# New begin times for the steady batch and the last batch of a planned adaLN kernel

## The chip, the cores and the metric

The kernel runs on one core of a Trainium2 chip. The metric is the device time of one execution in microseconds, median of 3 runs. Shorter is better.

## The reference, cut to what matters

The input is 8 batches of 1024 rows of 256 numbers. All of it is float32.

```python
mod = (silu(c) @ wmod).reshape(8, 6, 1, 256)      # sa, ca, ga, sb, cb, gb; |ga|, |gb| at least 0.25
h = layernorm(x) * (1 + ca) + sa
x = x + ga * causal_attention(h)                  # q, k, v by 16 small blocks, rope, softmax over 1024 keys
h = layernorm(x) * (1 + cb) + sb
y = h
for l in range(2):                                # two layers of the inner network
    q, k, v = split(shift_token(y) @ wqkv[l])     # 8 heads of 64
    q, k = xpos(l2norm(q) * qs[l], l2norm(k) * ks[l])
    y = y + window_attention(q, k, v) @ wo[l]     # own and previous 128 rows
    a, g = split(layernorm(shift_token(y)) @ w1[l] + b1[l])
    y = y + (a * gelu(g)) @ w2[l] + b2[l]         # 682 hidden units
x = x + gb * y
```

## The kernel before

The work of a batch is cut into tiles of 128 rows, 8 in a batch and 16 over its two layers. A **piece** is a short run of instructions of one kind on one engine for one tile, head group, pair of tiles or block of hidden units, and there are 9244 of them. The kinds that the text needs:

- `E` (TensorE, L508 and L514): one of the three 512-wide parts of q, k, v of a tile, six float16 matmuls. `ev` (ScalarE, L779) copies it out of PSUM. `Wg` and `Wa` (L613, L617) are the matmuls of the hidden layer, `J` (L594, L598) those of `wo`, `Y` (L160 to L162, L638) those of `w2`.
- `F` (L524) transposes q and k, float32 over all 128 rows of the array. `G` (L547, scores), `H` (L565, transposes of the probabilities) and `I` (L581, probabilities times v) are float32 matmuls that go to a part of the array, 64 rows or 64 columns of it.
- `x0` and `x1` (VectorE, L1079 and L1086): the two products of the position rotation, 128x1024, both operands in SBUF. `nm` (L1111, L1117) divides half of the probabilities by their sum, SBUF only. `ss` (L1054, L1059) sums squares. `yr` (L1183, and in layer 2 also L1188 and L1190) adds the result of `Y` to the residual; it is the last piece of a tile in a layer.
- `ad` (GpSimd, L1370) adds the two products, 128x1024. `pw` (L1366) raises a 128x16 block to the power -1/2, `kk` (L1376) scales k, 128x512, and `ul` (L1385) makes the low half of a hidden block, 128x512.
- `ex` (ScalarE, L808) and `pe` (L730) are exponentials, `ge` (L855) is the gelu. Going from one to the other loads another table.
- SyncE's queue issues all DMAs of the steady batches: `xl` loads two tiles of x (L310), `xs` writes shifted rows (L335, L337), `mb` and `mg` load gates, `os` stores a tile (L341).

The order of the pieces isn't written as a program. `BEGIN` holds a begin time for each piece of a batch, and a piece of batch b begins b times `PERIOD` later. `EDGE` replaces that time for single pieces of single batches, and `ONCE` holds the pieces of the set-up. `schedule()` sorts all pieces by time, engine by engine. That gives each engine its queue. At run time nothing waits for a clock: an engine takes the next piece of its queue as soon as the semaphores that the piece waits for have been counted up. A semaphore's target is the rank of the awaited piece in its own queue (`at()`). `plan_banks()` gives each TensorE piece the PSUM bank whose last use ends first by the same times, and TensorE waits for that use to end (`claim()`).

```python
time_b = round(time + b * PERIOD, 2)
made.append((EDGE.get((k, engine), {}).get(piece[1:], time_b), engine, piece))
```

In the steady state the queues hold two batches at once: the causal attention of batch b+1 lies among the pieces of the second layer of batch b.

Of the kernel before, what the change touches and what calls it, by code (L numbers as in the profile page):

```python
# [46 lines left out]
def adaln_kernel(nc, x, w_q, w_k, w_v, wqkv, q_scale, k_scale, wo, ln_g, ln_b, w1, b1, w2, b2,  # L47
# [3 lines left out]
    with ExitStack() as ctx:  # L51
# [1342 lines left out]
PERIOD = 316.98  # L1394
BEGIN = {
# [525 lines left out]
```

How the kernel before makes its waits and increments, by code:

```python
        def claim(pe, *use):  # L275
            for old in before[use]:
                pe.wait_ge(*empty(old))
            return bank[use]
# [12 lines left out]
        def root(pool, ve, mv, rs, lo, hi, s_eps, count):  # L292
            pool.tensor_scalar(ve[:, lo:hi], mv[:, lo:hi, 1], EPS, None, ALU.add).then_inc(s_eps, 1)
            pool.wait_ge(s_eps, count)
            return pool.tensor_tensor(rs[:, lo:hi], ve[:, lo:hi], neg_half[:, 0:hi - lo], ALU.pow)
# [5 lines left out]
            @block.sync  # L302
            def _(sp):
                for piece in ORDER["sp"]:
                    k = piece[0]
                    if k == "xl":
                        b, p = piece[1:]
                        if b:
                            sp.wait_ge(s_fin, (b - 1) * NT + 2 * p + 2)
                        sp.dma_start(X[:, 2 * p:2 * p + 2, :],
                                     x[b, 2 * p * P:(2 * p + 2) * P, :].rearrange("(t p) d -> p t d", p=P)
                                     ).then_inc(s_x[p], 16)
                    elif k == "mb":
                        b = piece[1]
                        if b:
                            sp.wait_ge(s_u0, at("lr", b - 1, NT - 1))
                        else:
                            sp.wait_ge(l_store, 16)
                        sp.dma_start(modb[:, :, :],
# [3 lines left out]
                        b = piece[1]  # L323
                        if b:
                            sp.wait_ge(s_fa, b * NT)
                        else:
```

## Time and profile before

| | us |
|---|---|
| median of 3 runs | 2638.1 |
| lowest and highest run | 2637.03, 2639.17 |
| span of the profiled execution | 2634.1 |
| TensorE busy in the span | 2526.7 |
| VectorE busy in the span | 2260.9 |
| ScalarE busy in the span | 1935.6 |
| GpSimd busy in the span | 1303.7 |

The span goes from the first to the last instruction of the profiled execution. The profile gives no device time of that execution beside its span. The median of the timed runs is 4.0 us above the span, and that is taken for what lies around it. Busy times of TensorE are modelled at their ends and overlap a little, so they say less than the starts of its instructions.

### The profile page before, as it was taken

How to read it: one execution, taken by the hardware profiler on the slowest of the kernel's cores; microseconds unless marked ns; L12 is line 12 of the kernel's file. 1: busy time of each engine (PE TensorE's matmuls, PEld its weight loads, DVE VectorE, ACT ScalarE, POOL GpSimd, SP SyncE). 2: the span in 40 equal slices, each digit the busy share in tenths (PEclk: the TensorE clock that was granted, in tenths of full speed). 3: DMA queues.
4: the chain of work that ended last, by engine and by line, in shares of the span. 5: the costliest groups of instructions: out<-in, count | busy, mean ns of one | idle time of the engine just before them, and what ended most of it. 6: DMA issues, size and time to landing. Idle time of an engine off the chain costs nothing.

```text
span 2634.1 us, 71297 instructions
## 1 busy us (share of the span) xinstructions
PE 2526.7 (96%) x25566; PEld 1725.1 (65%) x25566; DVE 2260.9 (86%) x6247; ACT 1935.6 (73%) x4782; POOL 1303.7 (49%) x953
## 2 busy tenths in 40 slices
PE   7899989999899998999999999999999999999998
PEld 4566666666567665676656666666766666666675
DVE  8997889878898788987889878998889978799785
ACT  3698856888478784788748787587874878658884
POOL 2364535555355554555436554365544555446552
PEclk8999999999999999999999999999999999999999
DMA  5000010000100000000000000000000000000000
GB/s 192 22 7 8 5 43 3 9 5 15 33 3 9 6 17 30 4 10 4 18 29 5 8 5 20 25 6 8 6 19 25 6 8 6 20 25 6 7 6 21
DMA packets 51021, 46.45 MB, mean 18 GB/s; under 512 B 11530, under 2 KB 47980, under 8 KB 50548
## 3 DMA queue, kind: packets, MB, share of 16 engines
q1 hardware_dynamic: 50004, 40.78, 5.0%
q8 instruction: 213, 3.49, 0.6%
q14 instruction: 132, 1.08, 0.1%
q10 hardware_dynamic: 672, 1.10, 0.1%
HBM read 25.06 MB, written 8.42 MB: 13 GB/s over the span
## 4 chain that ended last, share of the span: by engine, by line
PE 69%; DVE 12%; ACT 8%; issue 5%; POOL 4%; DMA 1%; SPq 1%; DVEq 0%; POOLq 0%; ACTq 0%
PE ps L508 10%; PE ps L613 9%; PE ps L581 8%; PE ps L547 6%; PE ps L514 5%; PE ps L617 4%; PE ps L565 4%; PE ps L524 3%; PE ps L594 3%; PE ps L160 2%; PE ps L162 2%; PE ps L161 2%; ACT ar_b L808 2%; PE ps L461 2%; PE ps L407 2%
## 5 line engine op out<-in xcount | busy, mean ns | idle before, releaser
L808 ACT ACTIVATE ar_b<-ar_b,small 128x192 f32<-128x192 f32 (+1 forms) x1024 | 445.2, 437 | 50.4 <-DVE small L1100 48.6
L1366 POOL TENSOR_TENSOR small<-small,neg_half 128x16 f32<-128x16 f32 x128 | 382.2, 2986 | 121.8 <-DVE small L1059 119.9
L1370 POOL TENSOR_TENSOR ar_c<-ar_c 128x1024 f32<-128x1024 f32 x128 | 302.7, 2365 | 282.3 <-DVE ar_c L1086 281.7
L1100 DVE CUSTOM_DVE_ANT_0 ar_b<-ps,mask_t,small 128x192 f32<-128x192 f32 x896 | 319.3, 413 | 29.7 <-PE ps L547 29.2
L1385 POOL TENSOR_TENSOR mlp<-mlp 128x512 f16<-128x512 f32 x160 | 196.3, 1231 | 200.5 <-ACT mlp L863 199.3
L508 PE MATMUL ps<-wqkv_hi,ht_hi 128*128 128x512 f16 x768 | 292.2, 381 | 0.0
L508 PE MATMUL ps<-wqkv_lo,ht_hi 128*128 128x512 f16 x768 | 291.1, 379 | 0.0
L613 PE MATMUL ps<-ht_hi,w_hi 128*128 128x512 f16 (+1 forms) x704 | 268.2, 381 | 5.5 <-ACT ht_hi L759 5.5
L613 PE MATMUL ps<-ht_hi,w_lo 128*128 128x512 f16 (+1 forms) x704 | 267.1, 379 | 0.0
L581 PE MATMUL ps<-ar_b,ar_a 128*64 128x128 f32 x3840 | 239.4, 276 | 0.5 <-DVE ar_b L1124 0.3
L294 POOL TENSOR_SCALAR stats<-stats 128x2 f32<-128x2 f32 x128 | 33.2, 260 | 407.6 <-DVE stats L1149 312.5
L514 PE MATMUL ps<-wqkv_hi,ht_lo 128*128 128x512 f16 x768 | 228.4, 379 | 0.0
L581 PEld LDWEIGHTS ps<-ar_b,ar_a 128*64 128x64 f32 x3840 | 207.2, 137 | 29.7 <-issue 17.4
L617 PE MATMUL ps<-ht_lo,w_hi 128*128 128x512 f16 (+1 forms) x704 | 209.9, 380 | 0.0
L1176 DVE SCALAR_TENSOR_TENSOR mlp<-ps,bias,mlp 128x512 f32<-128x512 f32 x192 | 142.5, 749 | 70.1 <-PE ps L617 33.1
L819 ACT ACTIVATE ar_b<-ar_b,rsw 128x192 f32<-128x192 f32 (+1 forms) x512 | 193.7, 441 | 11.2 <-DVE rsw L1111 10.2
L547 PE MATMUL ps<-ar_a 64*64 64x64 f32 (+2 forms) x5536 | 196.7, 282 | 2.8 <-ACT ar_a L798 2.8
L1124 DVE COPY ar_b<-ps 128x512 f32<-128x512 f32 (+1 forms) x256 | 160.2, 648 | 44.1 <-PE ps L565 44.1
L808 ACT ACTIVATION_READ_ACCUMULATOR ar_b<-ar_b,small 128x1 f32 x1024 | 193.4, 189 | 0.0
L547 PEld LDWEIGHTS ps<-ar_a 64*64 64x64 f32 x5536 | 153.4, 133 | 40.0 <-issue 22.6
L160 PE MATMUL ps<-w_hi,mlp 128*128 128x256 f16 x640 | 175.4, 274 | 0.2 <-POOL mlp L1385 0.2
L162 PE MATMUL ps<-w_hi,mlp 128*128 128x256 f16 x640 | 175.1, 274 | 0.0
(193 smaller groups left out, 6673.3 us busy)
## 6 DMA issues: line engine op xcount, KB each, us to landing
xu<-in_L_attn_x_dram SPq DMA_DIRECT2D x32, 256.0 KB, 2.8
out_dram<-xu SPq DMA_DIRECT2D x64, 128.0 KB, 2.4
rows<-xu SPq DMA_DIRECT2D x128, 63.5 KB
mlp<-in_L_ffn_wqkv_dram SPq DMA_DIRECT2D x2, 1536.0 KB, 6.4
modb<-mod_rows SPq DMA_DIRECT2D x8, 384.0 KB, 4.5
rows<-in_L_ffn_w_dram SPq DMA_DIRECT2D x2, 1364.0 KB, 9.5
rows<-xu SPq DMA_DIRECT2D x112, 0.5 KB
ar_b<-in_L_wmod_dram SPq DMA_DIRECT2D x2, 768.0 KB, 7.4
```

The costliest lines, as they stand in the source:

```text
L160: pe.matmul(o, a[0], b[0], start=start, stop=False)
L162: return pe.matmul(o, a[1], b[0], start=False, stop=stop)
L508: pe.matmul(ps[:, bk, :], ht[0][:, c, a:a + P], wqkv_p[i][:, L % DEPTH, c, s * INNER:(s + 1) * INNER], start=(c == 0 and i == 0), stop=False)
L514: last = pe.matmul(ps[:, bk, :], ht[1][:, c, a:a + P], wqkv_p[0][:, L % DEPTH, c, s * INNER:(s + 1) * INNER], start=False, stop=(c == 1))
L547: last = pe.matmul(ps[HQ * half:HQ * half + HQ, bk[q], i * KW + o:i * KW + o + m], QT[r:r + HQ, n % 2, hp, HQ * half:HQ * half + HQ], KT[r ...
L581: last = pe.matmul(ps[64 * q:64 * q + 64, bk, (h // 2) * P:(h // 2 + 1) * P], V[:, (n - 1 + kb) % 4, h * DH:(h + 1) * DH], PTW[:, f, q, 2 ...
L613: pe.matmul(ps[0:m, bk, :], q[:, L % DEPTH, c, 2 * j + i, 0:m], ht[0][:, c, a:a + 512], start=(c == 0 and q is w1_p[0]), stop=False)
L617: last = pe.matmul(ps[0:m, bk, :], w1_p[0][:, L % DEPTH, c, 2 * j + i, 0:m], ht[1][:, c, a:a + 512], start=False, stop=(c == 1))
L808: last = act.activation(pw, pw, ACT.Exp, bias=mnw[:, n % 2, h:h + 1], scale=-1.0, accum_out=smw[:, n % 2, h:h + 1])
L1100: dve.tensor_tensor_reduce(out=PW[:, pw_at(f, q, i) + c:pw_at(f, q, i) + KW], in0=ps[:, bk, i * KW + c:(i + 1) * KW], in1=mask, scale=rinv ...
L1366: pool.tensor_tensor(rinv[:, n % 4, :], ssm[:, n % 2, :], neg_half[:, 0:16], ALU.pow).then_inc(s_rinv, 1)
L1370: pool.tensor_tensor(M1[:, n % 2, :], M1[:, n % 2, :], M2, ALU.add).then_inc(s_add, 1)
```

## The change

All begin times are replaced: `PERIOD`, `BEGIN`, `ONCE` and `EDGE`. The set of pieces, the functions and the instructions in each piece stay as they are. The old tables begin at -30.17, the new ones at 0. `EDGE` had 709 times, all for the first batch and the first part of the second, and now has 2575, for the first batch, much of the second and the last one.

Sorted by time, the two tables give these queues. In the first batch they are the same up to the new time 328: the first 291 pieces of TensorE, 325 of ScalarE, 339 of VectorE, 106 of GpSimd and 32 of SyncE don't move. In a steady batch 252 of TensorE's 316 pieces and 296 of VectorE's 356 stand in another place among those of their batch, by at most 25 places, and in the last batch 268 and 313. SyncE's stores `os` stood together behind the four `xl` of the next batch, and now most of them stand between those.

The core of the diff (`EDGE` has keys with all numbers of a piece, `BEGIN` those within a batch):

```diff
-PERIOD = 316.98
+PERIOD = 320.36
 BEGIN = {
...
-    ("mg", "sp"): {(): 152.68},
...
-    ("os", "sp"): {0: 345.6, 1: 346.12, 2: 346.64, 3: 347.16, 4: 347.68, 5: 348.2, 6: 348.72, 7: 349.24},
...
-    ("xl", "sp"): {0: -23.25, 1: -1.62, 2: 23.79, 3: 28.11},
...
-    ("yr", "dve"): {0: 159.25, 1: 160.25, 2: 180.65, 3: 182.5, 4: 220.94, 5: 222.55, 6: 226.86, 7: 240.7, 8: 289.53,
-        9: 291.44, 10: 307.79, 11: 313.97, 12: 338.13, 13: 339.38, 14: 342.32, 15: 343.7},
...
+    ("mg", "sp"): {(): 72.74},
...
+    ("os", "sp"): {0: 337.97, 1: 340.58, 2: 356.01, 3: 358.81, 4: 386.82, 5: 389.25, 6: 390.55, 7: 393.53},
...
+    ("xl", "sp"): {0: 20.6, 1: 38.83, 2: 69.26, 3: 73.55},
...
+    ("yr", "dve"): {0: 204.11, 1: 205.81, 2: 211.51, 3: 223.3, 4: 265.83, 5: 267.94, 6: 270.01, 7: 273.27, 8: 336.56,
+        9: 339.17, 10: 354.6, 11: 357.4, 12: 385.41, 13: 387.84, 14: 389.14, 15: 392.12},
...
 EDGE = {
...
-    ("x0", "dve"): {(0,): 53.47, (1,): 63.85, (2,): 83.24, (3,): 93.24, (4,): 99.35, (5,): 117.53, (6,): 136.13,
-        (7,): 143.72, (8,): 171.4, (9,): 177.69, (10,): 195.38},
...
-    ("yr", "dve"): {(0,): 160.5, (1,): 161.12, (2,): 183.17, (3,): 183.5},
...
+    ("x0", "dve"): {(0,): 93.25, (1,): 104.41, (2,): 125.18, (3,): 135.67, (4,): 141.9, (5,): 160.49, (6,): 179.15,
+        (7,): 186.86, (8,): 215.69, (9,): 222.11, (10,): 239.86, (11,): 261.56, (12,): 276.17, (13,): 286.85,
...
+    ("yr", "dve"): {(0,): 205.16, (1,): 205.62, (2,): 227.38, (3,): 227.84, (4,): 265.96, (5,): 267.71, (6,): 272.06,
+        (7,): 285.69, (8,): 336.57, (9,): 339.18, (10,): 354.62, (11,): 357.41, (12,): 385.43, (13,): 387.85,
+        (14,): 389.15, (15,): 392.13, (16,): 524.38, (17,): 526.18, (18,): 531.88, (19,): 543.67, (20,): 586.2,
...
+        (31,): 712.49, (116,): 2511.26, (117,): 2513.96, (118,): 2529.58, (119,): 2530.74, (120,): 2590.5,
+        (121,): 2593.05, (122,): 2596, (123,): 2597.95, (124,): 2615.73, (125,): 2617.6, (126,): 2619.47,
+        (127,): 2621.34},
```

What else can be counted in the two sets of tables, before and after:

| counted in the tables | before | after |
|---|---|---|
| steps on TensorE from a piece of another kind to `G`, `H` or `I`, steady batch | 32 | 45 |
| the same in the interval of the last batch, and in all | 32, 257 | 51, 356 |
| table loads on ScalarE, steady batch, last batch, all | 14, 12, 112 | 12, 6, 94 |
| `nm`, `x0`, `x1` that overlap a `kk` or `ul` by the tables, steady batch | 14 | 6 |
| `nm`, `x0`, `x1` that overlap a `pw` by the tables, steady batch | 19 | 22 |

## Rows read from the trace of the kernel before

**Rows 1.** The page: span, busy time of each engine and the granted TensorE clock in 40 slices.
```profile
span 2634.1 us, 71297 instructions
...
PE 2526.7 (96%) x25566; PEld 1725.1 (65%) x25566; DVE 2260.9 (86%) x6247; ACT 1935.6 (73%) x4782; POOL 1303.7 (49%) x953
...
PEclk8999999999999999999999999999999999999999
```

**Rows 2.** The page: the chain of waits that ended last, share by engine.
```profile
PE 69%; DVE 12%; ACT 8%; issue 5%; POOL 4%; DMA 1%; SPq 1%; DVEq 0%; POOLq 0%; ACTq 0%
```

**Rows 3.** Windows, one steady batch and the last: PE, PEld, DVE, ACT, POOL, clock, DMA.
```profile
1348.00:1669.00 321.00, 311.06 (x3163) 212.30 (x3161) 278.12 (x774) 239.44 (x595) 162.85 (x118) 0.99 0.05 13
...
2311.00:2634.00 323.00, 305.54 (x3090) 207.20 (x3090) 262.20 (x720) 231.95 (x578) 155.17 (x109) 0.98 0.04 13
```

**Rows 4.** Timeline of VectorE: `x0` of tiles 0 and 8, then `yr`: start, duration.
```profile
91.23 1.23 DVE L1079 TENSOR_TENSOR ar_c<-ar_b,xp_t 128x1024 f32<-128x1024 f32 x1
...
211.55 1.22 DVE L1079 TENSOR_TENSOR ar_c<-ar_b,xp_t 128x1024 f32<-128x1024 f32 x1 [0.23 <-ACT ar_b L779]
...
281.60 0.41 DVE L1183 TENSOR_TENSOR xu<-ps,xu 128x256 f32<-128x256 f32 x1
...
281.93 0.16 DVE L1111 RECIPROCAL rsw<-small 128x4 f32<-128x4 f32 x1
...
385.68 0.42 DVE L1183 TENSOR_TENSOR xu<-ps,xu 128x256 f32<-128x256 f32 x1
...
2310.43 0.42 DVE L1183 TENSOR_TENSOR xu<-ps,xu 128x256 f32<-128x256 f32 x1
...
2630.57 0.42 DVE L1183 TENSOR_TENSOR xu<-ps,xu 128x256 f32<-128x256 f32 x1 [0.51 <-PE ps L638]
```

**Rows 5.** Timeline of VectorE and GpSimd at 1149 us.
```profile
1149.16 1.42 DVE L1117 TENSOR_TENSOR ar_b<-ar_b,rsw 128x384 f32<-128x384 f32 x1
...
1149.00 1.15 POOL L1385 TENSOR_TENSOR mlp<-mlp 128x512 f16<-128x512 f32 x1 [0.38 <-ACT mlp L863]
...
1150.12 3.23 POOL L1366 TENSOR_TENSOR small<-small,neg_half 128x16 f32<-128x16 f32 x1
```

**Rows 6.** Timeline of VectorE and GpSimd at 1138 us.
```profile
1138.33 1.23 DVE L1079 TENSOR_TENSOR ar_c<-ar_b,xp_t 128x1024 f32<-128x1024 f32 x1
...
1139.47 1.24 DVE L1079 TENSOR_TENSOR ar_c<-raw,xp_t 128x1024 f32<-128x1024 f32 x1
...
1138.41 3.91 POOL L1366 TENSOR_TENSOR small<-small,neg_half 128x16 f32<-128x16 f32 x1 [5.33 <-DVE small L1059]
```

**Rows 7.** By source line: durations in ns, least, median and most.
```profile
L1117 DVE TENSOR_TENSOR ar_b<-ar_b,rsw x256: 424/558/1419, 121.4 to 2586.5; 128x384 f32<-128x384 f32 x112, 128x256 f32<-128x256 f32 x16
...
L1385 POOL TENSOR_TENSOR mlp<-mlp x160: 1149/1159/2061, 184.2 to 2619.5; 128x512 f16<-128x512 f32 x160
...
L1366 POOL TENSOR_TENSOR small<-small,neg_half x128: 2892/2910/3907, 108.1 to 2560.4; 128x16 f32<-128x16 f32 x128
```

**Rows 8.** Groups by line and shape: busy us, mean ns of one.
```profile
L1117 DVE TENSOR_TENSOR ar_b<-ar_b,rsw 128x384 f32<-128x384 f32 x224 | 144.4, 644 | 7.8 <-DVE rsw L1111 0.2
```

**Rows 9.** Timeline of TensorE: where pieces `E` and what follows begin.
```profile
1414.20 0.38 PE L508 MATMUL ps<-wqkv_hi,ht_hi 128*128 128x512 f16 x1
...
1415.59 0.59 PE L565 MATMUL ps<-id_f,ar_b 64*128 64x64 f32 x12
...
1447.53 0.38 PE L508 MATMUL ps<-wqkv_hi,ht_hi 128*128 128x512 f16 x1
...
1448.82 0.38 PE L508 MATMUL ps<-wqkv_hi,ht_hi 128*128 128x512 f16 x1
...
1450.12 1.05 PE L524 MATMUL ps<-id_f,ar_c 128*128 128x128 f32 x8
```

**Rows 10.** By source line: the table loads that stand before `ge`.
```profile
L855 ACT ACT_TABLE_LOAD  x56: 1283/1283/1283, 176.4 to 2602.9; - x56
```

**Rows 11.** Waits of SyncE's queue: for whom, us in total, times, longest.
```profile
SPq L335 <- DVE xu L1136: 1952.9, 120, 65.1
```

More of the change, by code:

```diff
@@ L1391 @@
 BY_LAYER = ("D", "N", "Wg", "Wa", "dh", "dl", "nh", "nl", "ls", "lt", "lk", "ge", "us", "uh", "ul")
-PERIOD = 316.98
+PERIOD = 320.36
 BEGIN = {
[203 rows of a table removed]
[204 rows of a table added]
 }
 ONCE = {
-    ("bw", "pe"): {(0, 0): -7.46, (0, 1): 2.64, (0, 2): 8.25, (0, 3): 12.59, (1, 0): 40.81, (1, 1): 45.54,
-        (1, 2): 47.41, (1, 3): 48.84},
-    ("co", "act"): {(0,): -15.41, (1,): 27.89},
-    ("cq", "act"): {(0, 0): 2.68, (0, 1): 6.61, (1, 0): 45.3, (1, 1): 70.45},
-    ("cv", "act"): {(0,): -0.64, (1,): 46.67},
-    ("cw", "act"): {(0, 0): -6.21, (0, 1): 0.82, (1, 0): 31.73, (1, 1): 51.89},
-    ("do", "dve"): {(0,): -13.19, (1,): 29.82},
-    ("dq", "dve"): {(0, 0): 6.25, (0, 1): 8.34, (1, 0): 50.99, (1, 1): 103.49},
-    ("dv", "dve"): {(0,): 1.11, (1,): 85.3},
-    ("dw", "dve"): {(0, 0): 10.54, (0, 1): 21.57, (1, 0): 36, (1, 1): 60.87},
-    ("z0", "dve"): {(): -30.17},
-    ("zM", "pe"): {(): -21.4},
-    ("zR", "pe"): {(): -23.65},
-    ("zT", "pe"): {(): -27.43},
-    ("zW", "pe"): {(): -18.05},
-    ("za", "act"): {(): -30.17},
-    ("zb", "sp"): {(): -5.02},
-    ("zc", "sp"): {(): -29.7},
-    ("zd", "act"): {(): -22.56},
-    ("ze", "act"): {(): -26.54},
-    ("zf", "dve"): {(0,): 19.32, (1,): 53.25},
-    ("zg", "sp"): {(): -21.69},
-    ("zh", "act"): {(): -18.51},
-    ("zi", "dve"): {(): -26.32},
-    ("zk", "dve"): {(): -19.57},
-    ("zl", "dve"): {(): -17.64},
-    ("zm", "sp"): {(): -7.6},
-    ("zn", "dve"): {(): -17.81},
-    ("zo", "sp"): {(0,): -26.98, (1,): -26.5},
-    ("zp", "dve"): {(): -22.56},
-    ("zq", "sp"): {(0,): -7.3, (1,): 10.18},
-    ("zr", "act"): {(): -11.57},
-    ("zs", "sp"): {(): 10.7},
-    ("zt", "dve"): {(): -10.36},
-    ("zu", "dve"): {(): -20.44},
-    ("zv", "sp"): {(0,): -25.48, (1,): 16.46},
-    ("zw", "sp"): {(0,): -26.02, (1,): 23.63},
-    ("zx", "sp"): {(): -6.78},
-    ("zy", "dve"): {(0,): 31.55, (1,): 44.52},
-    ("zz", "dve"): {(): 79.71},
@@ new lines @@
+    ("bw", "pe"): {(0, 0): 24.44, (0, 1): 35.88, (0, 2): 42.36, (0, 3): 46.53, (1, 0): 76.74, (1, 1): 82.64,
+        (1, 2): 85.68, (1, 3): 88.28},
+    ("co", "act"): {(0,): 15.82, (1,): 63.1},
+    ("cq", "act"): {(0, 0): 37.32, (0, 1): 41.26, (1, 0): 82.28, (1, 1): 110.79},
+    ("cv", "act"): {(0,): 33.52, (1,): 83.76},
+    ("cw", "act"): {(0, 0): 28.48, (0, 1): 35.22, (1, 0): 69.39, (1, 1): 92.52},
+    ("do", "dve"): {(0,): 22.38, (1,): 65.6},
+    ("dq", "dve"): {(0, 0): 41.37, (0, 1): 43.29, (1, 0): 88.48, (1, 1): 146.27},
@@ new lines @@
+    ("dv", "dve"): {(0,): 35.71, (1,): 127.38},
+    ("dw", "dve"): {(0, 0): 45.77, (0, 1): 57.23, (1, 0): 71.78, (1, 1): 101.22},
+    ("z0", "dve"): {(): 0},
+    ("zM", "pe"): {(): 12.54},
+    ("zR", "pe"): {(): 11.04},
+    ("zT", "pe"): {(): 6.88},
+    ("zW", "pe"): {(): 16.04},
+    ("za", "act"): {(): 0},
+    ("zb", "sp"): {(): 32.11},
+    ("zc", "sp"): {(): 0.43},
+    ("zd", "act"): {(): 8.96},
+    ("ze", "act"): {(): 8.66},
+    ("zf", "dve"): {(0,): 54.92, (1,): 92.75},
+    ("zg", "sp"): {(): 8.48},
@@ new lines @@
+    ("zh", "act"): {(): 14.97},
+    ("zi", "dve"): {(): 9.07},
+    ("zk", "dve"): {(): 13.76},
+    ("zl", "dve"): {(): 16.67},
+    ("zm", "sp"): {(): 27.03},
+    ("zn", "dve"): {(): 16.32},
+    ("zo", "sp"): {(0,): 3.07, (1,): 3.55},
+    ("zp", "dve"): {(): 10.49},
+    ("zq", "sp"): {(0,): 27.33, (1,): 45.32},
+    ("zr", "act"): {(): 22.32},
+    ("zs", "sp"): {(): 45.97},
+    ("zt", "dve"): {(): 24.42},
+    ("zu", "dve"): {(): 12.16},
+    ("zv", "sp"): {(0,): 4.48, (1,): 52.77},
+    ("zw", "sp"): {(0,): 4.03, (1,): 59.44},
@@ L1643 @@
+    ("zx", "sp"): {(): 27.98},
+    ("zy", "dve"): {(0,): 67.43, (1,): 80.76},
+    ("zz", "dve"): {(): 121.28},
 }
 EDGE = {
[153 rows of a table removed]
[466 rows of a table added]
 }
```

1005 rows, old and new, of tables (BEGIN, EDGE) are left out of this document.

## Prediction

> **What bounds the kernel now.** I read the page first. Of the span of 2634.1 us TensorE is busy for 2526.7, at the higher of its two clock levels (2.4 GHz) in nearly every slice after the first, and VectorE for 2260.9 [rows 1]. The chain of waits says how much of the end each engine sets: TensorE 69%, VectorE 12%, ScalarE 8%, GpSimd 4% [rows 2]. The windows show that a steady batch keeps TensorE busy for 311 of 321 us and VectorE for 278, and that the last interval is less dense on all engines (305.5 and 262.2 of 323) though it is as long [rows 3]. So the kernel is near TensorE's own work in the middle and has room at its end.
>
> Then I compared the trace with the old table, by the begin of `yr` of a batch's last tile. The trace has it at 385.68 in batch 0, at 2310.43 in batch 6 and at 2630.57 in batch 7 [rows 4]. The period is (2310.43 - 385.68)/6 = 320.79 us, where the old table says 316.98. The old table is 3.81 us or 1.20% too quick per batch. The last interval is 2630.57 - 2310.43 = 320.14, and 3.5 us of span follow.
>
> **What the new table's own times are worth.** No instruction is added or removed, so the change is queues, bank choice and nothing else. The new table gives each piece a time, and that can be tested on the trace of before, because the first batch's queues are the same up to about 328. The new table has `x0` of tile 0 at 93.25, of tile 8 at 215.69, and `yr` of tile 7 at 285.69. The trace has them at 91.23, 211.55 and 281.60 [rows 4]. So the trace is 2.0, 4.1 and 4.1 us ahead of the new table. The old one (with its offset of 30.17) gives 83.64 and 270.87 for the first and the last of these, 7.6 and 10.7 us too early: it loses 3.1 us in 190.4, 1.63%, and 1.20% in the steady state. The new table gains 2.1 in 190.4, 1.1%, all of it before 212. One reason is visible: after `yr` of tile 7 VectorE begins the next instruction 0.33 us later [rows 4], the old table's shortest such step is 0.33 and the new one's is 0.46. The new table is a little slow on VectorE.
>
> **The sum.** It goes by four stretches of the span.
> 1. To `yr` of tile 15: 392.13 in the new table, less the lead of 4.1, is 388.0. Before it was 385.7. The 2.3 us are paid because the second batch's attention is interleaved otherwise near the end of batch 0.
> 2. Six periods of 320.36 plus an error d. The lead shows d between 0 (the flat stretch from tile 8 to `yr` 7) and -1.1% or -3.5 us (the whole stretch). I take the middle, -1.8, since either stretch is part of a batch.
> 3. The last interval: 2621.34 - (392.13 + 6 x 320.36 = 2314.29) = 307.05, against 320.14 before. By the same half rate that is -1.7. The gain of 13 us is the largest single term, and the room for it is in [rows 3].
> 4. The tail of 3.5 us stays.
>
> What the new table doesn't charge: a step from another kind to `G`, `H` or `I`. In the trace `E` at 1447.53 is followed by `E` at 1448.82 and by `F` at 1450.12, 1.29 and 1.30 us, but `E` at 1414.20 by `H` only at 1415.59, 1.39 us [rows 9]. The new table gives all of these 1.30. The same undercharge is in the calibrated first batch with its 32 to 35 such steps, so only the added ones count: 13 in a steady batch, 19 in the last. At 0.095 us, and with TensorE on 69% of the chain [rows 2], that is +0.85 and +1.25.
>
> So d = -1.8 + 0.85 = -0.95, a period of 319.4. Total: 388.0 + 6 x 319.4 + (307.05 - 1.7 + 1.25 = 306.6) + 3.5 = 2614.5 us of span, 19.6 less than before. With the 4.0 us between span and median this is 2618.5, and I say 2619 us, 0.72% faster. Carrying no lead forward at all (d = +0.85, last 308.3) gives 2621.9 + 4.0 = 2626. This end, too, is faster.
>
> **The contention.** `nm` at 1149.16 takes 1.42 us while `ul` runs on GpSimd from 1149.00 for 1.15, and the `pw` behind it, begun at 1150.12, takes 3.23 [rows 5]. The medians are 0.56 and 2.91 [rows 7]. `nm` of the 384-wide form has a mean of 644 against a median of 558 ns, 0.086 x 224 = 19.3 us in all or 2.4 per batch [rows 7, 8]. By the tables 14 of the `nm`, `x0` and `x1` of a batch overlap a `kk` or `ul` before, and 6 after. If all of 2.4 went and all lay on the path, a period would lose 2.4; if only VectorE's 12% share counted, 0.3. I take none of it on top: the first batch, on which the table was tested, had such stretches in its measured times, and the table's 320.36 already supposes them gone. That the steady state has fewer than the batch it is tested on speaks for the lower half of my range.
>
> Here a rule of the Trainium skill is to be weighed, from the page "SBUF — State Buffer", section "SBUF: two separate sides": VectorE with two SBUF inputs and GpSimd share a port pair as an exclusive lock for the whole instruction, and who comes second fully blocks. For `ul` and `nm` the trace agrees: `nm` starts 0.16 after `ul` and takes 0.86 more than its median, about the rest of `ul`. For `pw` it doesn't: `x0` at 1139.47 runs wholly inside a `pw` begun at 1138.41 and takes 1.24 us, its usual time; it is `pw` that takes 3.91 instead of 2.91, having begun behind another `x0` [rows 6, 7]. By the rule the change would keep its worst case, since overlaps of `nm`, `x0` and `x1` with `pw` go from 19 to 22 in a batch. By the trace they cost VectorE nothing and `pw` at most 1.0 us each.
>
> **Edits that I cost at nothing.** The shift of all times by 30.17 changes no queue. Two table loads fewer per steady batch and six fewer in the last take 2 x 1.28 and 6 x 1.28 us off ScalarE [rows 10], but the new times have them already; uncovered they would be worth 8% of that. SyncE's stores go ahead of loads in its queue. A store waits for the `yr` that the load behind it also waits for, and the queue mostly idles (1952.9 us before the `xs` alone, [rows 11]), so the load loses one issue. If the cover goes, it is `st` and the first LayerNorm of the next batch that are late, by about a microsecond per batch, +7 in all. `mg` waits for the whole previous batch and stands before the last `xl` now. What is queued behind it waits for nearly the same `yr`. Bank waits change everywhere, and I have no row for them; they cost between nothing and the late case of the first rival.
>
> **Rivals.**
> - *TensorE is the bound and its undercharge is paid in full: slower.* All 45 steps to `G`, `H`, `I` cost 0.095, 4.3 us per batch, and nothing that the table overcharges gives it back: period 324.6, last interval 307.05 + 51 x 0.095 = 311.9, total 388.0 + 1947.6 + 311.9 + 3.5 + 4.0 = 2655. For it: 311 of 321 busy. Against it: the first batch has the same undercharge and is ahead of the table all the same. It decides from an error of +1.9 us in each of the seven intervals, where the gain is gone: (2634.1 - 388.0 - 1922.2 - 307.05 - 3.5)/7.
> - *The queues don't do what the table says: no change.* Engines start when semaphores allow, orders tuned to times that are off by a per cent meet waits that the table hasn't, and the tail keeps its length of 320: 388.0 + 6 x 320.4 + 320 + 3.5 + 4.0 = 2638. For it: the old table missed its last interval by 3 us and each period by 3.8.
> - *The table is slow everywhere.* The lead grows by 1.1% in every batch: period 320.36 - 3.5 + 0.85 = 317.7, last 307.05 - 3.4 + 1.25 = 304.9, total 388.0 + 1906.2 + 304.9 + 7.5 = 2607. For it: the old table did better in the steady state (1.20%) than in the tested stretch (1.63%).
> - *Full blocking at `pw`*, each `pw` shutting out VectorE's SBUF pieces: three more overlaps per batch and 1.7 us more of them by the tables, on the path at most 1.7 x 8 = 14 us, so 2626 + 14 = 2640. Against it stands [rows 6]. The Trainium skill page "SBUF — State Buffer" would have it so.
>
> **Chances.** My forecast (2612 to 2631) 0.55; the slow table, down to 2600, 0.18; no change 0.14; TensorE bound 0.10; blocking 0.03. A measurement of this kernel tells 0.2% (5.3 us) from no change. Faster: 0.55 + 0.18 and a share of the rest, 0.76. Same: 0.13. Slower: 0.11. The range of 2602 to 2640 leaves out the TensorE case and the far end of the slow-table case; the forecast's own range is 2612 to 2631.
>
> **What would show it.** In the profile after, `yr` of tile 15 near 388, batches 319 to 320 us apart, the last interval near 307, the mean of L1117 near its median, and 94 table loads. `E` before `H` should still take 1.39. Wrong would be a period over 322.3, or a last interval over 315; then I should look at what TensorE waits for.

## The result, and the profile after

| | before | after |
|---|---|---|
| median of 4 runs, us | 2637.6 | 2820.7 |
| ratio, 95% interval | | 1.0695 [1.0679, 1.071] |
| `yr` of tile 15, batch 0 | 385.68 | 395.33 |
| period, batches 1 to 6 | 320.8 | 348.6 |
| last interval | 320.1 | 329.7 |

The change makes the kernel 7% slower. I had said 0.7% faster, and 2820.7 lies far outside the range of 2602 to 2640. The error of 202 us is the first batch (+7.3), six periods of 348.6 where 319.4 was said (+175), the last interval (+23), and 3 us less around the span than I took.

The page of after, as [rows 1] and [rows 2]:

```profile
span 2819.9 us, 71279 instructions
...
PE 2587.5 (92%) x25566; PEld 1725.6 (61%) x25566; DVE 2359.5 (84%) x6247; ACT 1930.4 (68%) x4764; POOL 1320.7 (47%) x953
...
PEclk8999999999999999999999999999999999999999
...
PE 57%; DVE 23%; issue 8%; DMA 6%; ACT 3%; POOL 2%; SPq 1%; DVEq 0%; POOLq 0%; ACTq 0%
```

The matmuls and VectorE's counted instructions are the same in number, but VectorE is busy 98.6 us longer and TensorE 60.8. VectorE holds 23% of the chain instead of 12, and DMA 6% instead of 1.

The windows of after, one steady batch and the last interval, as [rows 3], with the same columns:

```profile
1440.50:1788.30 347.80, 318.80 (x3161) 212.16 (x3161) 292.28 (x773) 239.49 (x593) 165.55 (x118) 0.99 0.04 12
2486.70:2816.40 329.70, 307.66 (x3079) 203.96 (x3078) 269.20 (x711) 223.27 (x568) 152.47 (x106) 0.99 0.03 9
```

TensorE idles 29 us in a steady batch, where it was 10. VectorE does its work of a batch in 292 us and not 278: instructions that don't wait in the queue take longer.

VectorE's timeline of after, `yr` of the last tile of batches 0, 6 and 7, as [rows 4]:

```profile
395.33 0.42 DVE L1183 TENSOR_TENSOR xu<-ps,xu 128x256 f32<-128x256 f32 x1
...
2486.70 0.42 DVE L1183 TENSOR_TENSOR xu<-ps,xu 128x256 f32<-128x256 f32 x1
...
2816.38 0.42 DVE L1183 TENSOR_TENSOR xu<-ps,xu 128x256 f32<-128x256 f32 x1 [0.51 <-PE ps L638]
```

**First reading: a wait that I had not priced.** VectorE's waits, for whom, us in total, times, longest. After:

```profile
DVE stats L1145 <- DMA rows<-xu: 68.5, 36, 4.7
```

Before:

```profile
DVE stats L1145 <- DMA rows<-xu: 8.8, 17, 2.0
```

L1145 is the second half of `ls`, the statistics of the inner LayerNorm for two tiles. It reads the rows that `xs` has shifted. VectorE's timeline of after at such a place, start, duration, wait in brackets:

```profile
1612.75 0.42 DVE L1136 TENSOR_TENSOR xu<-ps,xu 128x256 f32<-128x256 f32 x1
1613.20 0.49 DVE L1142 BATCH_NORM_STATS2 stats<-xu 128x6 f32<-128x128 f32 x2
1618.35 0.49 DVE L1145 BATCH_NORM_STATS2 stats<-rows 128x6 f32<-128x128 f32 x2 [4.66 <-DMA rows<-xu]
```

and SyncE's queue in the same microseconds:

```profile
1613.19 0.60 SPq L335 DMA_DIRECT2D rows<-xu  x1
```

The residual `jr` (L1136) ends at 1613.17, `xs` is issued at once, and the rows can be read at 1618.35, 5.2 us behind `jr`. The trace of before has the same time: its 17 waits at L1145 end 5.16 to 5.26 us behind the last `jr`, the 36 of after 5.16 to 5.66. By the old table the least distance from the second `xs` to `ls` is 4.71 us in a steady batch. By the new one four of eight are well below it: 2.51, 2.52, 3.91 and 4.20. The new table moves `ls` nearer to its DMA than the DMA takes, and VectorE stands.

**Second reading: SBUF pieces of VectorE under `ad`.** VectorE's timeline of after, three places:

```profile
1479.31 1.31 DVE L1059 TENSOR_SCALAR small<-small 128x16 f32<-128x16 f32 x1
...
1505.57 2.38 DVE L1039 SCALAR_TENSOR_TENSOR xu<-xu,stats,modb 128x256 f32<-128x256 f32 x1
...
1517.17 2.73 DVE L1117 TENSOR_TENSOR ar_b<-ar_b,rsw 128x384 f32<-128x384 f32 x1
```

GpSimd's timeline of after, the same places:

```profile
1478.23 2.36 POOL L1370 TENSOR_TENSOR ar_c<-ar_c 128x1024 f32<-128x1024 f32 x1 [9.83 <-DVE ar_c L1086]
...
1505.15 2.52 POOL L1370 TENSOR_TENSOR ar_c<-ar_c 128x1024 f32<-128x1024 f32 x1 [4.41 <-DVE ar_c L1086]
...
1517.13 2.36 POOL L1370 TENSOR_TENSOR ar_c<-ar_c 128x1024 f32<-128x1024 f32 x1 [8.28 <-DVE ar_c L1086]
```

L1059 (the clip behind the sums of squares) takes 0.17 us elsewhere, L1039 (the last step of a LayerNorm's output) 0.48 and L1117 0.56. Each began while an `ad` (L1370) ran and ended 0.03 to 0.41 us behind its end. I summed, over all groups of VectorE instructions of one line and shape, what each takes above the median of its group. This **stretch** is 141 us in after and 49 in before: L1117 45.6 (before 19.3), L1059 32.7 (8.4), L1039 26.6 (0.5), L1016 9.3 and L1190 6.1 (both 0). Not all of it is `ad`'s. Put down to the GpSimd instruction that ran beside each, 84 us of the 141 fall to `ad` (before 9), and L1016 and L1190 were stretched beside two other GpSimd pieces, the subtraction `hl` (L1343) and the addition `ra` (L1348). In each steady batch seven instructions are blocked by `ad` for over half a microsecond, at the same places every time: three L1059, two L1039 and two L1117. With smaller ones that makes 12.2 us a batch, where it was 1.2. The prediction weighed `nm` (L1117) under `ul` and `pw`. It never asked about `ad`.

**Third reading: TensorE pays for a wait twice.** L1039 at 1505.57 is such a block, and TensorE waits for it. TensorE's timeline of after around it:

```profile
1504.73 0.38 PE L508 MATMUL ps<-wqkv_lo,ht_hi 128*128 128x512 f16 x1
...
1508.00 0.72 PE L407 MATMUL ps<-id_f,xu 128*128 128x128 f32 x4 [2.46 <-DVE xu L1039]
...
1510.12 0.63 PE L508 MATMUL ps<-wqkv_lo,ht_hi 128*128 128x512 f16 x1
```

Windows of TensorE there (stretch, length, busy, granted clock and DMA):

```profile
1508.00:1509.60 1.60, 1.60 (x12) 0.64 0.00 0
1509.70:1512.00 2.30, 2.30 (x8) 0.53 0.03 7
1512.00:1516.00 4.00, 4.00 (x28) 1.00 0.00 0
```

TensorE had been busy for 4.5 of the 7.9 us up to 1507.9, with 2.46 us of idling at their end. Behind that the granted clock is 0.64 and then 0.53, about the lower of the two levels (1.2 GHz), and a matmul of 0.38 us takes 0.63. That is part of TensorE's 60.8 us. It doesn't follow each time: behind the same stall of 2.46 us at 812.7 the granted clock stays at 1.00. Over the whole span the clock is 0.978, where it was 0.987. An estimate from these two shares is 0.022 x 2819.9 - 0.013 x 2634.1 = 28 us of full-speed time, if TensorE was at work in all of it.

### The profile page after: what moved, and what is told of

It is laid out like the page before. It is cut to its first block, busy times and chain, and to the rows that moved or that the text cites. A ratio compares the mean times of both kernels' runs of the same rounds, so it can differ in the third digit from the quotient of the medians.

```text
span 2819.9 us, 71279 instructions
## 1 busy us (share of the span) xinstructions
PE 2587.5 (92%) x25566; PEld 1725.6 (61%) x25566; DVE 2359.5 (84%) x6247; ACT 1930.4 (68%) x4764; POOL 1320.7 (47%) x953
## 4 chain that ended last, share of the span: by engine, by line
PE 57%; DVE 23%; issue 8%; DMA 6%; ACT 3%; POOL 2%; SPq 1%; DVEq 0%; POOLq 0%; ACTq 0%
PE ps L613 10%; PE ps L581 7%; PE ps L508 6%; DMA rows<-xu 5%; PE ps L617 5%; PE ps L547 4%; PE ps L565 4%; PE ps L594 3%; PE ps L514 3%; PE ps L524 2%; PE ps L160 2%; PE ps L162 2%; PE ps L161 2%; PE ps L461 2%; DVE ar_c L1086 2%
## 5 line engine op out<-in xcount | busy, mean ns | idle before, releaser
L1370 POOL TENSOR_TENSOR ar_c<-ar_c 128x1024 f32<-128x1024 f32 x128 | 304.9, 2382 | 455.3 <-DVE ar_c L1086 454.2
L581 PE MATMUL ps<-ar_b,ar_a 128*64 128x128 f32 x3840 | 247.0, 278 | 6.5 <-ACT ar_b L827 6.1
L565 PE MATMUL ps<-id_f,ar_b 64*128 64x64 f32 x3840 | 167.7, 228 | 41.3 <-DVE ar_b L1117 20.4
L565 PEld LDWEIGHTS ps<-id_f,ar_b 64*128 64x128 f32 x3840 | 139.6, 139 | 105.7 <-DVE ar_b L1117 53.9
L1117 DVE TENSOR_TENSOR ar_b<-ar_b,rsw 128x384 f32<-128x384 f32 (+1 forms) x256 | 184.7, 721 | 9.1 <-DVE rsw L1111 0.4
```

The costliest lines, as they stand in the source:

```text
L565: last = pe.transpose(ps[:, bk[half], o:o + HQ], PW[r:r + HQ, c:c + P], id_f[r:r + HQ, r:r + HQ])
L581: last = pe.matmul(ps[64 * q:64 * q + 64, bk, (h // 2) * P:(h // 2 + 1) * P], V[:, (n - 1 + kb) % 4, h * DH:(h + 1) * DH], PTW[:, f, q, 2 ...
L1370: pool.tensor_tensor(M1[:, n % 2, :], M1[:, n % 2, :], M2, ALU.add).then_inc(s_add, 1)
```

## The experiments

The base was measured beside each group of runs, at 2638.8 to 2640.1. Most edits were put into the new kernel and, as a control, into the old one. All figures are medians of 4 to 10 runs. What a run is less than after is taken from the one median of 2820.7, measured beside a base of 2637.6, so such a difference is uncertain by 2 or 3 us.

### The wait for the shifted rows

In `stats_u` the second half of `ls` reads the unshifted columns, and the wait moves to `lk`, the next reader. The shift's part in the statistics is left out.

```diff
-                        dve.wait_ge(s_xs[l * 4 + p], 16 * (4 - (p == 0)) * (b + 1))
...
-                            last = dve.bn_stats(stw[:, w, 1, :], XS[:, w, :])
+                            last = dve.bn_stats(stw[:, w, 1, :], U[:, w, P:DIM])
...
+                        dve.wait_ge(s_xs[L % DEPTH * 4 + p], 16 * (4 - (p == 0)) * (L // DEPTH + 1))
```

> The kernel after, but ls takes the second half of its statistics from U instead of the shifted rows (so the sums are of other numbers), waits for no DMA, and lk waits for the rows instead, at least 2.1 us later in the table. Queues unchanged. DMA-wait theory: VectorE stops 68.5 us in all before L1145 because seven of eight ls lie less than 5.5 us behind their xs; most of that goes and the time falls by 60 to 140 us, to 2680 to 2760. Lock theory (small SBUF pieces of VectorE shut out by GpSimd's ad): the blocked 141 us of VectorE stay, and the time falls by 10 us at most. TensorE theory (more steps to G, H, I): no change within 5 us.

> The same edit on the kernel before, as the control. VectorE stops 8.8 us in all before L1145 there, so the DMA-wait theory gives 0 to 9 us less, 2629 to 2638; the others give no change.

Measured 2774.7 in the new kernel, 46.0 less, and 2635.4 in the old one, ratio 0.9983 [0.9974, 0.9992]. The stretch in the new kernel stays at 144 us. So the wait is real and about a quarter of the loss of 183 us (a part of it may only have moved to `lk`); my figure for it was too high.

The mirror of it puts only the early `ls` into the old table, and leaves nothing out:

```diff
+    for L in range(NB * DEPTH):
+        for p in range(NT // 2):
+            t = when["xs", L * NT + 2 * p + 1][0] + 2.5
+            when["ls", L, p][0] = min(when["ls", L, p][0], round(t, 2))
```

> The kernel before with each ls set to at most 2.5 us behind its second xs (old table: 4.7 to 11.6), nothing else. DMA-wait theory: about eight stops of 2.2 us or more per batch on VectorE, 18 us per batch, of which 12% (VectorE's share of the chain before) to all is paid: 2655 to 2780. Lock theory and TensorE theory: within 5 us of 2638.

Measured 2783.6, 1.0536 [1.0519, 1.0554]: 144 us lost by the place of one kind of piece. Its waits:

```profile
DVE stats L1145 <- DMA rows<-xu: 119.8, 64, 2.9
```

That is 111 us more than before, and the stretch stays (45 us). In VectorE's queue each `ls` of a steady batch stands 1 to 11 places further ahead. So a microsecond of VectorE's standing costs more than a microsecond here (144 for 111).

The other way round, `ls` a little later in the new table, to 4.9 us behind `xs` where the place of `lt` (GpSimd, the next step of the same LayerNorm) allows it:

```diff
...
+            t = when["xs", L * NT + 2 * p + 1][0] + 4.9
+            lt, ls = when["lt", L, p], when["ls", L, p]
+            ls[0] = max(ls[0], min(round(t, 2), round(lt[0] - 0.02, 2)))
```

> The new kernel, whole, with one change of order: where the planned time from the second xs to ls is under 4.9 us, ls begins later, up to 4.9 us behind xs but ahead of lt's planned time (in the steady batch four of eight ls move, by 0.2 to 1.25 us; the others keep their place). Theory A: VectorE does other pieces in some of the time that it stood waiting, 5 to 35 us less than after. Rival B: each ls still waits, for lt's planned time caps the shift, and the time stays within 5 us.

Measured 2821.3, the time of after. Its waits are unchanged:

```profile
DVE stats L1145 <- DMA rows<-xu: 67.5, 36, 4.7
```

This run tests neither theory, for its edit does nearly nothing. Only the order counts at run time, and sorted by time the two queues of VectorE differ in one exchange in the whole run (`ls` and `yr` next to each other in batch 0) and in no steady batch; the other four queues are the same. The new begin times pass no other piece. It is in effect a second measurement of after, 0.6 us from the first. Whether an `ls` that is really placed later wins something back in the new order was not tried.

### The block under `ad`

`ad` on 64 of its 1024 columns. The second product of the rotation is left out in the others.

```diff
-                        pool.tensor_tensor(M1[:, n % 2, :], M1[:, n % 2, :], M2, ALU.add).then_inc(s_add, 1)
+                        pool.tensor_tensor(M1[:, n % 2, 0:64], M1[:, n % 2, 0:64], M2[:, 0:64], ALU.add).then_inc(s_add, 1)
```

> The new kernel with `ad`, GpSimd's rotary addition, on 64 of its 1024 columns, so that the long instruction of 2.36 us (L1370) that VectorE's small pieces stood under becomes a short one; the other 960 columns stay without the second rotary product. Theory A (the wait of ls for the shifted rows and the block by ad add up to most of the slowdown): VectorE's stretch over its usual durations falls from 141 to about 60 us and the time falls by 60 to 120 us, to 2700 to 2760. Rival B (the wait for the rows and the delay it hands on are the cause, and the block by ad is hidden): the time falls by no more than 20, to 2800 or above. The control before_ad_short says what the shorter work alone gives.

> The control: the same cut of ad to 64 columns in the kernel before. Theory A: VectorE's stretch there is 49 us and only part of it under ad, so 0 to 15 us less than before. Rival B: the same; if it falls by over 30, the cut is worth something by itself and the fall of after_ad_short has to be read against it.

Measured 2753.3 in the new kernel, 67.5 less, and 2643.1 in the old one, 1.0012 [1.0003, 1.0022]. In the old order the shorter work gives nothing. The source lines in the new kernel with short `ad`, with least, median and greatest duration in ns:

```profile
L1039 DVE SCALAR_TENSOR_TENSOR xu<-xu,stats,modb x64: 483/485/487, 53.2 to 2487.5; 128x256 f32<-128x256 f32 x64
```
```profile
L1059 DVE TENSOR_SCALAR small<-small x128: 174/175/222, 108.4 to 2681.9; 128x16 f32<-128x16 f32 x128
```

The same lines in after:

```profile
L1039 DVE SCALAR_TENSOR_TENSOR xu<-xu,stats,modb x64: 483/485/2396, 54.0 to 2550.7; 128x256 f32<-128x256 f32 x64
```
```profile
L1059 DVE TENSOR_SCALAR small<-small x128: 174/175/1843, 108.7 to 2751.1; 128x16 f32<-128x16 f32 x128
```

The stretch falls from 141 to 55 us, with nothing left under `ad` but 0.3 us a batch. Of the terms that were taken out, this is the largest. The edit does two things at once: it takes the block away, and it makes `ad` itself 2.0 us shorter (0.32 us in place of 2.36) for what waits for its sum. In the old order neither is worth anything; how the 67.5 us divide between them in the new order was not separated. That the block as such reaches TensorE is seen at 1508.00, where TensorE waits for a blocked L1039, and in the next run, which leaves `ad` as it is.

One victim alone, the clip L1059, is taken out; it is all that is left out:

```diff
-                        dve.tensor_scalar(ssm[:, n % 2, :], ss[:, n % 2, :], 1e-24, None, ALU.max).then_inc(s_rm, 1)
-                        pool.tensor_tensor(rinv[:, n % 4, :], ssm[:, n % 2, :], neg_half[:, 0:16], ALU.pow).then_inc(s_rinv, 1)
+                        pool.tensor_tensor(rinv[:, n % 4, :], ss[:, n % 2, :], neg_half[:, 0:16], ALU.pow).then_inc(s_rinv, 1)
```

> The new kernel without the clip at L1059 (ss clipped from below at 1e-24), a VectorE piece of 0.17 us that was stretched by 32.7 us in sum over the run (before: 8.4); pw reads the sums directly. It leaves out the clip alone. Theory A: 15 to 45 us less, since the stretch of this piece goes with it and 128 pieces of 0.17 us (22 us) too. Rival B: 10 us less or fewer. Rival C: no change, the block moves to the piece that then stands at that place.

> The kernel before without the clip at L1059; it leaves out the clip alone. It is the control of after_noclip, which came out 24 us under the new kernel, and a candidate for a version below both. The piece was stretched by 8.4 us in sum in before, and 128 x 0.17 = 22 us of VectorE's work go with it, most of it beside TensorE: 2 to 12 us less, 2627 to 2637. If TensorE alone sets the period here, 0.

Measured 2796.8 in the new kernel, 23.9 less, and 2637.6 in the old one, 0.9995 [0.9986, 1.0005]. 128 instructions of 0.17 us are worth nothing in the old order, where they were stretched by 8.4 us in all, and 24 us in the new one, where it was 32.7, most of it under `ad` (28). The stretch falls by 31 us, so the block doesn't move to the next piece.

### Both, and what is left

> The new kernel with both causes taken out at once: ls reads its second half from U's own tile (no wait for the shifted rows) and ad is cut to 64 columns. Theory A: the two account for nearly all of the slowdown, 2640 to 2680. Rival B (there is a third cause, such as TensorE's own work standing too close in the new table): 2700 or above.

Measured 2705.3: 115.5 less than after, and 46.0 + 67.5 = 113.5, so the two add up. But 2705 is not 2640 to 2680: there is more. VectorE's timeline of this kernel shows a part, a wait that has only moved:

```profile
1549.87 0.28 DVE L1148 BATCH_NORM_AGGREGATE stats<-stats 128x2 f32<-128x12 f32 x2
1554.21 0.35 DVE L1158 TENSOR_SCALAR rows<-xu,stats 128x128 f32<-128x128 f32 x1 [4.06 <-issue]
```

`lk` (L1158) now waits for the same rows; their `jr` ended at 1548.94, again 5.3 us earlier. So `lk` too was made to read the unshifted columns:

> The new kernel with ad on 64 of 1024 columns, ls and lk both reading U's own columns (the copy of shifted rows is still issued, and only yr, at least 15 us later, asks for it). It leaves out the shift by one row and most of ad. In after_both, where only ls had stopped waiting for the rows, VectorE still stood 4.1 us in each steady batch ahead of an lk. Theory A (that wait is the remainder of the wait for the rows and holds up TensorE): 25 to 40 us less than after_both, 2665 to 2680. Rival B (it lies beside TensorE's work, and a third cause holds the rest): within 10 us of after_both, 2695 to 2710.

Measured 2701.2, 4 less, where I had expected 25 to 40. Those 4 us per batch lay beside TensorE's work. Then all long GpSimd pieces but `pw` were cut (the others from the second batch on):

> The same, and from the second batch on all of GpSimd's long pieces are short: hl on 32 of 256 columns, ra, ad and ul on 64 columns, kk on one head of eight; pw stays as it is. It leaves out those columns of the subtractions, additions and products. With it nothing of GpSimd's can stand under VectorE for long and no row is awaited. Theory A (contention and the rows are all of the slowdown, the new table's spacing is otherwise sound): 2610 to 2650, near the prediction's 2619. Rival B (TensorE's spacing in the new table costs by itself): 2660 or above.

> The control, the same edit in the kernel before, which had 52 us of VectorE stretch, only part of it under these pieces, and 9 us of waits for rows. Theory A: 10 to 30 us less than before, 2608 to 2628, so that the two tables come within 30 us of each other. Rival B: the same here, and the new table stays over 40 us above it.

Measured 2678.3 and 2626.6. The stretch is 21 us in both, and VectorE's work of a steady batch is the same (275.7 and 274.5 us), yet the new table is still 51.7 us behind. Its period is 327.7, where the old table has 319.8 (319.5 in the batch shown). Windows of a steady batch, first the new kernel, then the old one, both with this edit:

```profile
1377.50:1705.20 327.70, 314.26 (x3160) 211.20 (x3160) 275.73 (x773) 239.27 (x593) 87.97 (x118) 0.99 0.04 13
```
```profile
1347.80:1667.30 319.50, 310.51 (x3160) 212.72 (x3160) 274.47 (x773) 239.65 (x595) 87.28 (x118) 0.99 0.05 13
```

In these batches the new table keeps TensorE busy 3.8 us longer, and idle 4.4 us longer. Part of the first is what the prediction called the undercharge. TensorE's timeline of the new kernel with this edit, an `E` and the `H` after it:

```profile
1599.68 0.39 PE L508 MATMUL ps<-wqkv_hi,ht_hi 128*128 128x512 f16 x1
...
1601.09 0.72 PE L565 MATMUL ps<-id_f,ar_b 64*128 64x64 f32 x16
```

That is 1.41 us where the new table has 1.30 (it was 1.39 in [rows 9]). The old table gives this step 1.39, so there it is planned for. In a steady batch 48 steps, nearly all to or from `G`, `H` and `I`, take 0.07 to 0.13 us longer than the new table has them, 4.3 us in sum.

How much of TensorE's own time counts was measured by taking some away: the second of two matmuls of the third product of `Wg` for half of the blocks, 12 of 88 per batch.

```diff
-                        for c in range(NC):
+                        some = k == "Wg" and j < 3
+                        for c in range(NC - some):
```

> after_no_xs_pool with 12 of the 88 L617 matmuls of each batch left out besides (the second half of the third product of Wg for three of its six column blocks), 12 x 0.379 = 4.5 us less of TensorE's work per batch, 36 in all. In after_no_xs_pool 48 steps of a steady batch from one kind of piece to G, H or I took 0.09 us longer than the table has them, 4.3 us per batch. Theory C (with the other causes out, TensorE's own work sets the period, so that this undercharge is paid in full and stays): 30 to 36 us less, 2642 to 2648. Rival D (waits between engines set the period, and TensorE's undercharge lies beside them): under 18 less, over 2660.

> The control, the same 12 matmuls per batch out of before_no_xs_pool. Theory C has the old table bound by TensorE at least as much (311 of 320 us busy), so 25 to 36 less, 2591 to 2602. Rival D: under 18 less.

Measured 2661.4 and 2608.9: 16.9 and 17.7 less.

What these are to be held against isn't the 36.4 us that I had expected from a duration of 0.379. Matmuls overlap, and the time that one takes from TensorE is the distance from start to start. TensorE's timeline of the new kernel before this edit:

```profile
1499.77 0.38 PE L613 MATMUL ps<-ht_hi,w_hi 128*106 128x512 f16 x1
1499.98 0.38 PE L613 MATMUL ps<-ht_hi,w_lo 128*106 128x512 f16 x1
...
1501.07 0.38 PE L613 MATMUL ps<-ht_hi,w_hi 128*128 128x512 f16 x1
```

One matmul begins 0.21 us behind the other, and a piece of six takes 1.30 us. The pieces that lost one take 1.08. So the 96 matmuls are 96 x 0.216 = 20.7 us of TensorE, and 0.82 and 0.85 of that came off the time. With 0.216 theory C reads 17 to 21 us in the new kernel and 14 to 21 in the old one, and rival D under 10. The runs (16.9 and 17.7) lie at the edge of C and in it, though by the bounds as they were written they would be D's. So with the row waits and long GpSimd pieces out, most of TensorE's own time is paid in either table, and the undercharge is worth about 4.3 x 0.82 = 3.5 us per batch (an estimate from this run).

### The last interval

The old tables up to the new time 2446, and from there the new one, shifted by 69.0; the computation is whole.

```diff
+    for q, (time, g) in new.items():
+        made.append((round(time - 69.0, 2) if time > 2446.0 else old[q][0], g, q))
```

> The old tables up to the new time 2446 and the new table, 69 us earlier, behind that: the last batch alone is set anew. If the new last batch keeps what its times say, the gain of 13 us is there: 2625. If waits and locks eat it as in the steady batches (lock and DMA-wait theory), 2633 to 2650: the last interval after was 329.7 against 320.1 before, of which its first part is the steady table's.

Measured 2640.8, 0.9999 [0.999, 1.0008]. Only what begins behind 2446 is moved, the last 175 us; by the tables the end comes 10.2 us earlier with it. The last interval is 321.3 us long, where before has 320.1. VectorE waits in it for shifted rows for 6.8 us (before 2.8), once for 4.7. The two kernels without row waits and long GpSimd pieces say the same of the whole interval: 314.2 us with the new table and 314.3 with the old one. The denser order wins nothing on the chip.

## Why the prediction was wrong

| kernel | us | below after | stretch |
|---|---|---|---|
| after | 2820.7 | | 141 |
| no clip | 2796.8 | 23.9 | 110 |
| `ls` doesn't wait for the rows | 2774.7 | 46.0 | 144 |
| `ad` short | 2753.3 | 67.5 | 55 |
| both of the last two | 2705.3 | 115.5 | 54 |
| and `lk` doesn't wait | 2701.2 | 119.6 | 54 |
| and `hl`, `ra`, `kk`, `ul` short | 2678.3 | 142.4 | 21 |
| the same in before | 2626.6 | | 21 |

- **The step that failed: the worth of the new times.** I took a table whose first batch the trace kept within 4.1 us as right for the steady state, to within d between 0 and -3.5. The steady batches have other queues than the first, so that test said nothing of their distances. The period came out 29.2 above what was said. With row waits and long GpSimd pieces out it was 327.7, so 20.9 of the 29.2 went with these two (and with the shorter work of GpSimd that the edit brings along), and 8.3 are left with the table itself. The error d, put at 0 to -3.5 and with 0.85 added, is the term of the sum that was wrong: it came out at +28.2.
- **What stood in its place, first:** the wait for the shifted rows. It had no term in the sum. One look at the distance from each `xs` to its `ls` in both tables, beside the 5.2 us that the trace of before already shows, would have found it. I counted order changes of SyncE's queue and not the landing of its DMAs.
- **Second: contention.** The prediction had the right mechanism at `ul` and the right finding at `pw` (after it too, `x0` isn't stretched there), but counted only `nm`, `x0` and `x1` against `kk`, `ul` and `pw`. What the change worsened is VectorE's SBUF pieces against `ad`, `nm` among them: 12.2 us of stretch in a steady batch. By the new table, with the offsets and durations that the trace shows, they overlap with `ad` for about 1.5 us a batch (an estimate), and by the old one for 0.8. The mean of the 384-wide L1117 was to come near its median of 0.56 us; it rose from 0.644 to 0.685. A piece put close to an `ad` of 2.4 us tips into it when one of the two is late by little; that is argued from the tables and the timeline, and no run moved such a piece alone. The rows' wait isn't needed for it: the stretch stays at 144 us when `ls` no longer waits.
- **The Trainium skill's rule** ("SBUF — State Buffer", section "SBUF: two separate sides"), of one exclusive lock per instruction and the second to come blocked in full, holds at `ad`: 2.38 us for a 0.48 us piece with two inputs in SBUF, ended 0.28 behind the `ad`. I had seen it hold at `ul` and fail at `pw`, and then gave a chance (0.03) to blocking at `pw` alone. It is the mechanism of the largest term, with another GpSimd piece than the one I named.
- **The last interval.** The gain of 13 us, the largest single term, was not there: 329.7 in after, 321.3 when the last 175 us of it were put into the old kernel, and 314.2 against the old table's 314.3 with rows and GpSimd out of the way. Rival 2, "the queues don't do what the table says", gave 320, but no change for the whole kernel.
- **TensorE's undercharge** was mis-sized as 0.85 us per batch, by the argument that the calibrated stretch contains it. The 48 steps are 4.3 us, of which about 3.5 count. `E` before `H` takes 1.39 to 1.41, as said. Rival 1 had the mechanism and priced it at 4.3 in full, which is near; alone it would have given 2655.
- **The first batch** came out at 395.33 and not 388.0. Up to about 350 the trace stayed ahead of the table, as in the calibration; the loss begins where the second batch's pieces are mixed in, with a wait of `ls` (1.7 us) among the first.
- **What was costed at nothing and cost nothing visible:** two loads fewer on ScalarE per batch, seen as 47 loads before `ge` (56 in [rows 10]). Stores and `mg` in SyncE's queue don't show among what ended VectorE's waits in the steady batch.
- **What stays open.** Of the 8.3 us per batch that the table itself is slower than forecast, about 2.7 are the undercharge (3.5 less 0.85) and 1.8 the lead that I carried forward. The other 3.8 are not shown. The trace has many short waits there (TensorE on `ar_b` of L1002 2.7, on `rows` of L1159 2.4, on `ht_hi` of L702 1.8), none of which I took out alone, and the changed choice of PSUM banks wasn't tried by itself. The version in which blocked pieces or `ls` are only placed elsewhere in the new order, with the whole computation, is missing as well. With the whole computation no version here beats the old kernel.
- **A slip in the sum.** With no lead carried forward, 388.0 + 6 x 321.21 + 308.3 + 3.5 + 4.0 is 2631, and not 2626: six times 0.85 was left out. The blocking rival, built on it, would be 2645 and lie outside the range. At 2820.7 it changes nothing.

## What to carry to other kernels

A planned order is only as good as the latencies it was planned with: before trusting its total, list for every DMA the distance from issue to first reader, and compare it with the trace. A stretch that a change doesn't alter can't vouch for the stretch that it does. When pieces are moved away from one long GpSimd instruction, look at which others they now stand beside, and leave room for lateness, not for the planned times. Price a matmul by the distance to the next start, not by its duration. And before a new begin time is measured, sort both tables: if no piece passes another, nothing is tested.

## What the hardware showed that I had not expected

- Copying 127 rows of 512 bytes from SBUF to SBUF took 5.2 us from the end of the producing instruction to the first read (median of 53 waits in before and after, 5.16 to 5.66). The loads of 256 KB from HBM landed in a median of 3.3 us in the same batch and the stores of 128 KB in 2.5.
- A VectorE instruction of 128x16 with one input (0.17 us) took up to 1.84 us under GpSimd's addition, while `pw`, also on GpSimd and longer (2.9 us), hardly stretches VectorE's: 1.7 of the 141 us in after ran beside it.
- TensorE idle for 2.46 us at 1505.5 was followed by a granted clock of 0.64 and 0.53 up to 1512.0, with matmuls of 0.63 in place of 0.38 us. The same stall at 812.7 was followed by 1.00.
- A float16 matmul of 512 columns is shown with 0.38 us and takes 0.216 from start to start.
